# DLRM tower: eight of 26 embedding fields looked up by one-hot matmuls, the other gathers in bursts of three, set-up, moment and layer order rebuilt

## The chip, the cores and the metric

The kernel runs on one core of a Trainium2 chip. The metric is the device time of one execution in microseconds, lower is better; the median of several runs is compared.

## The reference

For a batch of 512 rows, 26 embedding rows of 32 floats each are fetched from 26 tables (1,000 to 125,000 rows long), and pass two layers of a compressed interaction network and a small multilayer perceptron, all in float32:

```python
e = stack([tbl_f[ids[:, f]] for f in range(26)], axis=1)        # (512, 26, 32)
x1 = einsum('bik,bjk,hij->bhk', e, e, W1) + b1                    # h = 128
x2 = einsum('bik,bjk,hij->bhk', x1, e, W2) + b2                   # h = 128
z = sum(concat([x1, x2], axis=1), axis=-1)                        # (512, 256)
h = maximum(concat([z, dense_ctx], axis=1) @ W_top1 + b_top1, 0)  # 272 -> 512
h = maximum(h @ W_top2 + b_top2, 0)                               # 512 -> 256
y = h @ W_top3                                                    # 256 -> 1
```

Only the sum over the 32 embedding columns is needed, so z is a cubic form of the 26 fields. The kernel uses that: it sums products of three fields over k ("moments") and multiplies them with folded weights.

## The kernel before

The batch is worked in 4 tiles of 128 rows. A tile's 26 fields are fetched by 26 indirect DMAs (gathers) that GpSimd issues one after the other (L242), each 128 rows of 128 bytes, into the one tile `rows`. The fields form three parts (`PARTS`: 13, 10 and 3 fields). Each gather of part p waits for `s_turn[p]`: VectorE must have taken that part of the tile before out of `rows`, since there is one buffer.

VectorE then (`half_a`, `half_b`) transposes each part in 32x32 blocks into `prod` (L616), so that partitions hold (row quad, k), and multiplies pairs of fields: 14 instructions for the pairs within the first 13 fields and the mixed groups (`products_a`, L771 to L777), 8 for the pairs of the other 13 (`products_b`, L788). ScalarE spreads the fields into the block-diagonal tile `diag` (`fill_diag`, L467), four copies for each part, one for each 32 partitions.

TensorE forms the moments (`moments`, L321 and L322): for each of 32 groups of four rows one matmul of 108 columns and one of 64, stationary `prod`, moving `diag`. Four groups make a step, eight steps a tile; two pairs of PSUM banks take turns, and ScalarE (`copy_moments`, L485 to L489) and VectorE (`steps`, L650) copy each step out into `t0` and `t1` before the step after the next may start. Then come Z2 (`z2_b`, `z2_second_chunk`, `z2_a`: 13, 8 and 13 matmuls of 128 columns) and Z1 (5 matmuls), and the layers `mlp1` (12 matmuls), `mlp2` (8) and `mlp3` (2). Layer 2 and 3 of a tile run behind the moments of the next one. Tiles 1 to 3 are run by a hardware loop (`Fori`) on TensorE and VectorE, tiles 1 and 2 on ScalarE, and GpSimd's loop has two rounds of two tiles.

Ahead of the first moments stands the set-up, done once: W2 is transposed (L275), multiplied with W1's symmetrised pairs (L281, 26 matmuls of 183 columns) and with its mixed block (L287, 26 of 169), the products are added into `folded` (L662, 95 additions on VectorE), and `folded` is transposed into `v0` and `v1` (L299, L302). It runs beside the gathers of tile 0.

What sets the order of the work is the order in which each engine's program is written, and semaphores. These lines of the loop matter for the prediction:

```python
for f in range(f0, f1):
    pool.indirect_dma_start(rows[:, f, :], None, tables[f], ...).then_inc(s_got[part], 16)
...
dve.wait_ge(s_mom, t * STEPS + STEPS)   # half_a: all moments of the tile before
fields_in(t, 0)
```

## Time and profile before

| | us |
|---|---|
| median of 3 runs | 188.49 (187.81 to 188.94) |
| span of the profiled execution | 269.0 |
| its TensorE, busy | 171.1 |
| its ScalarE, busy | 103.7 |
| its VectorE, busy | 94.1 |
| its GpSimd, busy | 109.4 (104 gathers: 108.7) |

The profile is of another execution than the three timed ones, and its span is 80.5 us longer than their median; its own time outside of the recording is not among the numbers. So its durations of single instructions and its waits have to be read apart. PE is TensorE, PEld its weight loads, DVE VectorE, ACT ScalarE, POOL GpSimd, SP the queue engine. A float32 matmul stands as two records.

### The profile page before, as it was taken

Reading aid. Unit: us, or ns where it says so; the run is one execution under the profiler, and the core shown is the slowest. Engines: PE = TensorE matmul, PEld = TensorE weight load, DVE = VectorE, ACT = ScalarE, POOL = GpSimd, SP = SyncE. Lnnn points to the kernel's source line nnn. Section 1 sums busy time; section 2 is a strip of 40 time slices with the busy share of each in tenths; the row PEclk is TensorE's granted clock in tenths of the full one; section 3 lists DMA queues with packets and bytes.
Section 4 is the critical chain, followed back from the end, with each engine's and each line's share of the span. In section 5 each row is a group of like instructions: output and inputs, shape, how many; then the busy total and the mean of one; then the engine's idle time right before and its main releaser. Section 6 shows DMA issues by size and latency. Waiting matters only on the chain.

```text
span 269.0 us, 3544 instructions
## 1 busy us (share of the span) xinstructions
PE 171.1 (64%) x1239; PEld 158.7 (59%) x1239; DVE 94.1 (35%) x370; ACT 103.7 (39%) x267; POOL 109.4 (41%) x110
## 2 busy tenths in 40 slices
PE   7900594209929388986300799954001999899997
PEld 7800583209729287976300789954002999888985
DVE  0576003210943086920000568500003569047200
ACT  1020330019595165494000462951003463966313
POOL 3778777720077400577774003877770000000000
PEclk9975598556997869996555599995555799999999
DMA  6700011000001000011000000001000000000000
GB/s 240 250 12 13 12 14 14 13 7 0 0 10 17 11 1 4 2 12 15 14 12 10 0 0 2 11 12 15 12 12 2 0 0 0 0 0 0 0 0 3
DMA packets 5729, 5.08 MB, mean 19 GB/s; under 512 B 2875, under 2 KB 5061, under 8 KB 5718
## 3 DMA queue, kind: packets, MB, share of 16 engines
q0 software_dynamic: 3328, 1.71, 4.7%
q1 hardware_dynamic: 1698, 2.34, 2.6%
q10 hardware_dynamic: 692, 0.89, 1.0%
q8 instruction: 6, 0.10, 0.2%
q14 instruction: 5, 0.04, 0.1%
HBM read 4.93 MB, written 0.00 MB: 18 GB/s over the span
## 4 chain that ended last, share of the span: by engine, by line
PE 35%; another core or an unknown queue 30%; ACT 15%; DVE 9%; issue 9%; POOL 0%; DVEq 0%; ACTq 0%; POOLq 0%
PE bank L321 9%; ACT diag L467 8%; PE bank L287 4%; DVE t L650 4%; PE bank L322 4%; PE bank L281 4%; PE bank L256 3%; PE bank L332 2%; DVE prod L771 2%; PE bank L372 1%; ACT w2t L432 1%; ACT t L486 1%; DVE prod L616 1%; PE bank L275 1%
## 5 line engine op out<-in xcount | busy, mean ns | idle before, releaser
L242 POOL DMA_INDIRECT rows<-in_tbl_dram,idx x104 | 108.7, 1045 | 91.1 <-DVE prod L616 57.4
L321 PE MATMUL bank<-diag,prod 128*128 128x108 f32 x256 | 60.7, 336 | 56.0 <-DVE t L650 44.3
L321 PEld LDWEIGHTS bank<-diag,prod 128*128 128x128 f32 x256 | 46.6, 227 | 59.5 <-issue 59.5
L650 DVE COPY t<-bank 13x64 f32<-13x64 f32 (+2 forms) x128 | 26.7, 209 | 108.6 <-ACT t L487 66.7
L322 PE MATMUL bank<-diag,prod 128*77 128x64 f32 x256 | 41.7, 249 | 0.3 <-issue 0.3
L322 PEld LDWEIGHTS bank<-diag,prod 128*77 128x77 f32 x256 | 36.8, 173 | 0.5 <-issue 0.5
L485 ACT COPY t<-bank 55x128 f32<-55x128 f32 x32 | 8.3, 259 | 71.9 <-remote 47.8
L467 ACT COPY diag<-prod 32x416 f32<-32x416 f32 (+2 forms) x48 | 33.4, 696 | 1.0
L287 PE MATMUL bank<-w1ab,w2t 128*128 128x169 f32 x52 | 16.0, 489 | 14.6 <-ACT folded L434 9.7
L287 PEld LDWEIGHTS bank<-w1ab,w2t 128*128 128x128 f32 x52 | 12.8, 278 | 17.5 <-ACT folded L434 10.4
L281 PE MATMUL bank<-w1s,w2t 128*128 128x183 f32 x52 | 10.8, 377 | 16.4 <-ACT w2t L432 15.6
L281 PEld LDWEIGHTS bank<-w1s,w2t 128*128 128x128 f32 x52 | 10.3, 233 | 16.9 <-ACT w2t L432 15.8
L788 DVE TENSOR_TENSOR prod<-prod 128x364 f32<-128x364 f32 x32 | 16.5, 536 | 0.8
L489 ACT COPY t<-bank 128x432 f32<-128x432 f32 x32 | 16.4, 512 | 0.0
L434 ACT COPY folded<-bank 128x366 f32<-128x366 f32 x13 | 5.8, 469 | 25.8 <-remote 11.7
L662 DVE TENSOR_TENSOR folded<-folded 128x6 f32<-128x6 f32 (+15 forms) x44 | 5.1, 177 | 27.4 <-ACT folded L434 13.2
L662 DVE TENSOR_TENSOR folded<-folded,ct 128x52 f32<-128x52 f32 (+13 forms) x51 | 11.6, 301 | 7.4 <-ACT ct L437 7.3
L349 PE MATMUL bank<-t,v 128*128 128x128 f32 x104 | 12.7, 279 | 0.0
L332 PE MATMUL bank<-t,v 128*128 128x128 f32 x104 | 12.4, 276 | 0.3 <-ACT t L489 0.3
L332 PEld LDWEIGHTS bank<-t,v 128*128 128x128 f32 x104 | 11.9, 192 | 0.6 <-ACT t L489 0.6
L349 PEld LDWEIGHTS bank<-t,v 128*128 128x128 f32 x104 | 11.9, 192 | 0.5
L363 PE MATMUL bank<-z,wt 128*128 128x128 f32 x64 | 9.0, 286 | 2.8 <-issue 2.1
(79 smaller groups left out, 186.3 us busy)
## 6 DMA issues: line engine op xcount, KB each, us to landing
rows<-in_tbl_dram,idx POOLq DMA_INDIRECT x104
wt<-in_W_top_dram SPq DMA_DIRECT2D x2, 512.0 KB
w<-in_L_rec_W_dram ACTq DMA_DIRECT2D x1, 832.0 KB
w<-in_L_rec_W_dram SPq DMA_DIRECT2D x1, 832.0 KB
w<-in_L_rec_W_dram SPq DMA_DIRECT2D x1, 338.0 KB
idx<-in_ids_dram SPq DMA_DIRECT2D x4, 13.0 KB
vec<-in_L_rec_b_dram ACTq DMA_DIRECT2D x2, 0.5 KB
dctx<-in_dense_ctx_dram ACTq DMA_DIRECT2D x1, 32.0 KB
```

The lines of the kernel that those rows point to most:

```text
L242: pool.indirect_dma_start(rows[:, f, :], None, tables[f], bass.IndirectOffsetOnAxis(ap=idx[i][:, f:f + 1], axis=0)).then_inc(s_got[part], 16)
L281: mm = nc.tensor.matmul(ps[:, i * PAIRS:(i + 1) * PAIRS], w2t[:, x0 + i, :], w1s[:], start=True, stop=True)
L287: mm = nc.tensor.matmul(ps[:, i * HALF * HALF:(i + 1) * HALF * HALF], w2t[:, lo + x0 + i, :], rhs, start=True, stop=True)
L321: nc.tensor.matmul(m0[:, g * P:g * P + JW * QUADS], prod[:, G, 0:P], mov, start=True, stop=True)
L322: mm = nc.tensor.matmul(m1[0:M1, g * J1 * QUADS:(g + 1) * J1 * QUADS], prod[:, G, P:P + M1], mov[:, JLOW * QUADS:], start=True, stop=True)
L332: nc.tensor.matmul(Z2[:, 0:P], v0[:, j, :], t0[:, j, :], start=j == HALF, stop=False)
L349: mm = nc.tensor.matmul(Z2[:, 0:P], v0[:, j, :], t0[:, j, :], start=False, stop=j == HALF - 1)
L467: nc.scalar.copy(diag[q, :, f0:f1, r], prod[q, :, col:col + f1 - f0]).then_inc(s_diag, 1)
L489: nc.scalar.copy(dst(t0, 0, P, slice(0, JW)), view(m0, P, slice(0, JW), P)).then_inc(s_e0, 1)
L650: ins = nc.vector.tensor_copy(t1[p0:p0 + HALF, GRAM + slot:GRAM + slot + nb, n].rearrange("p j (g r) -> p j g r", r=QUADS), m1[64:64 + HAL ...
L662: ins = nc.vector.tensor_tensor(dest, dest, term[second], ALU.add)
L788: return eng.tensor_tensor(dst, left, right, ALU.mult)
```

## The change

- **Fields.** The 26 fields are put in another order. Eight of them, with tables of 1,000 or 1,250 rows, are no longer gathered. Their tables are loaded whole into SBUF (`small`, 1.15 MB, in chunks of 128 rows). A one-hot matrix of the index's low seven bits is made once for all 512 rows (8 matmuls of 512 columns that broadcast the indices, 8 comparisons on VectorE). For each tile, 8 matmuls (5 of 256 columns, 3 of 320) pick a row from every chunk (`look_up`), and VectorE picks the chunk: six multiplications with a 0/1 mask out of PSUM and six reductions (`pick`).
- **Gathers.** 18 for each tile remain, 72 in all, each tile with a buffer of its own; nothing waits for VectorE any more. GpSimd waits after every three until they have landed.
- **Set-up.** W2 comes in the transposed layout and W1 in the pair layout from the host (layout only, the additions stay on chip), so the transposes of W2, W1 and the context and most small additions into `w1s` go. Loads on the SP and ACT queues grow: W1 in pair layout 0.53 MB, its transposed form 0.66 MB, `small` 1.15 MB.
- **Moments.** Steps of 8 groups (4 steps) on two sets of three banks. One operand of the pair products is read from PSUM (`factor`).
- **Order.** No hardware loops. Each tile runs moments, Z2, Z1 and all three layers before the next tile's moments. The copies of `v0`'s low half stand behind tile 0's moments. ScalarE spreads over all 128 partitions at once with a scale that is 1 on one quarter (4 instructions for each of parts 0 and 1; VectorE does part 2).

```diff
-GSTEP = 4
+GSTEP = 8
+ORDER = [2, 6, 7, 9, 0, 1, 3, 4, 5, 8, 10, 11, 12, 16, 23, 24, 25, 13, 14, 15, 17, 18, 19, 20, 21, 22]
+PARTS = [(0, 13, COL_A, 4), (13, 23, COL_B, 17), (23, 26, COL_B + 10, 23)]
+LATE_PART = 2
+BURST = 3
+SMALL = [0, 1, 2, 3, 13, 14, 15, 16]
+CHUNKS = [8, 8, 8, 8, 8, 10, 10, 10]
+MAXC = max(CHUNKS)
+SPLACE = [EMB * sum(CHUNKS[:e]) for e in range(len(SMALL) + 1)]
+PICKS = [(0, 2), (2, 4), (4, 5), (5, 6), (6, 7), (7, 8)]
...
-            with nc.gpsimd.Fori(0, TILES // 2) as u:
-                for i in range(2):
-                    pool.wait_ge(s_idx[i], u * 16 + 16)
-                    for part, (f0, f1, _) in enumerate(PARTS):
-                        pool.wait_ge(s_turn[part], u * 2 + i + 1)
-                        pool.sem_inc(s_go, 1)
-                        for f in range(f0, f1):
-                            pool.indirect_dma_start(
-                                rows[:, f, :], None, tables[f],
-                                bass.IndirectOffsetOnAxis(ap=idx[i][:, f:f + 1], axis=0)).then_inc(s_got[part], 16)
+            for t in range(TILES):
+                if t < 2:
+                    pool.wait_ge(s_idx[t], 16)
+                for part, (_, f1, _, g0) in enumerate(PARTS):
+                    for f in range(g0, f1):
+                        if f > g0 and (f - g0) % BURST == 0:
+                            pool.wait_ge(s_got[t][part], 16 * (f - g0))
+                        pool.indirect_dma_start(
+                            rows[t][:, f, :], None, tables[f],
+                            bass.IndirectOffsetOnAxis(ap=idx[:, t, f:f + 1], axis=0)).then_inc(s_got[t][part], 16)
+                    pool.wait_ge(s_got[t][part], 16 * (f1 - g0))
...
+            def broadcast():
+                pe.wait_ge(s_place, 1)
+                for e in range(len(SMALL)):
+                    nc.tensor.matmul(bank[e][:], with_dims(ident[0:len(SMALL), e:e + 1], (0, P)), placef[:],
+                                     start=True, stop=True).then_inc(s_bc, 1)
+            def look_up(t, picks):
+                for pick in picks:
+                    e0, e1 = PICKS[pick]
+                    ps = bank[ARRIVE[t > 0][pick]]
+                    if t == 0 and pick >= 2:
+                        pe.wait_ge(s_pick, pick - 1)
+                    elif t and pick == 5:
+                        pe.wait_ge(s_pick, t * len(PICKS) + 1)
+                    for e in range(e0, e1):
+                        c = slice(SPLACE[e] - SPLACE[e0], SPLACE[e + 1] - SPLACE[e0])
+                        mm = nc.tensor.matmul(ps[:, c], onehot[:, e, t * P:(t + 1) * P],
+                                              small[:, SPLACE[e]:SPLACE[e + 1]], start=True, stop=True)
+                    mm.then_inc(s_em, 1)
...
+            def keep_clock(t):
+                pe.wait_ge(s_turn[1], t + 1)
+                for _ in range(FILL):
+                    nc.tensor.matmul(bank[2][:, 0:P], ident[:], ident[:], start=True, stop=True)
+            for t in range(TILES):
+                if t:
+                    pe.wait_ge(s_y, t)
+                if t == TILES - 1:
+                    keep_clock(t)
+                moments(t)
+                if t < TILES - 1:
+                    pe.wait_ge(s_e0, t * STEPS + 3)
+                    pe.wait_ge(s_eg, t * STEPS + 3)
+                    look_up(t + 1, (0, 1))
+                pe.wait_ge(s_e0, t * STEPS + STEPS)
+                pe.wait_ge(s_eg, t * STEPS + STEPS)
+                if t == 0:
+                    for q in range(DONE["v1"], len(SETUP)):
+                        make(q)
+                    pe.wait_ge(s_sf, len(SETUP))
+                    pe.wait_ge(s_vec, 32)
+                    pe.wait_ge(s_wt, 48)
+                if t < TILES - 1:
+                    look_up(t + 1, (2, 3, 4))
+                z2_low()
+                if t < TILES - 1:
+                    look_up(t + 1, (5,))
+                z2_high()
+                if t == 0:
+                    pe.wait_ge(s_z1w, 1)
+                z1()
+                if t < TILES - 1:
+                    pe.wait_ge(s_pick, (t + 2) * len(PICKS))
+                layer1(t)
+                layer2(t)
+                layer3(t)
...
-            def fill_diag(t, parts):
-                act.wait_ge(s_mom, t * STEPS + STEPS)
-                for part in parts:
-                    f0, f1, col = PARTS[part]
-                    act.wait_ge(s_turn[part], t + 2)
-                    for r in range(QUADS):
-                        q = slice(32 * r, 32 * r + 32)
-                        nc.scalar.copy(diag[q, :, f0:f1, r], prod[q, :, col:col + f1 - f0]).then_inc(s_diag, 1)
+            def spread(t, part):
+                f0, f1, col, _ = PARTS[part]
+                act.wait_ge(s_turn[part], t + 1)
+                for r in range(QUADS):
+                    ins = nc.scalar.activation(diag[:, :, f0:f1, r], prod[:, :, col:col + f1 - f0], ACT.Identity,
+                                               scale=quad[:, r:r + 1])
+                ins.then_inc(s_diag, 1)
+            for q in range(DONE["v1"]):
+                take(q)
+            for part in range(LATE_PART):
+                spread(0, part)
+            for t in range(TILES):
+                evict(t)
+                if t == 0:
+                    for q in range(DONE["v1"], len(SETUP)):
+                        take(q)
+                    act.wait_ge(s_vec, 32)
+                if t < TILES - 1:
+                    spread(t + 1, 0)
+                act.wait_ge(s_z2, t + 1)
+                nc.scalar.activation(z[1][:], Z2[:, 0:P], ACT.Identity, bias=b2x32[:, 0:1]).then_inc(s_z2s, 1)
+                act.wait_ge(s_z1, t + 1)
+                nc.scalar.copy(z[0][:], Z1[:, 0:P]).then_inc(s_z1s, 1)
+                relu1(t)
+                relu2(t)
+                copy_y(t)
+                if t < TILES - 1:
+                    spread(t + 1, 1)
...
+            for e in range(len(SMALL)):
+                dve.wait_ge(s_bc, e + 1)
+                nc.vector.tensor_scalar(onehot[:, e, :], bank[e][:], placef_of[:, 0:1], None,
+                                        ALU.is_equal).then_inc(s_oh, 1)
...
+            def pick(t):
+                if t == 0:
+                    dve.wait_ge(s_ch, 1)
+                for i, (e0, e1) in enumerate(PICKS):
+                    n, cs = e1 - e0, CHUNKS[e0]
+                    width = n * EMB * cs
+                    dve.wait_ge(s_em, t * len(PICKS) + i + 1)
+                    if t or i:
+                        dve.wait_ge(s_sum, t * len(PICKS) + i)
+                    nc.vector.tensor_tensor(
+                        picked[:, 0:width].rearrange("p (f k c) -> p f k c", f=n, c=cs),
+                        bank[ARRIVE[t > 0][i]][:, 0:width].rearrange("p (f k c) -> p f k c", f=n, c=cs),
+                        with_dims(chosen[:, t, e0, 0:1], (MAXC, n), (0, EMB), (1, cs)), ALU.mult).then_inc(s_pick, 1)
+                    dve.wait_ge(s_pick, t * len(PICKS) + i + 1)
+                    nc.vector.tensor_reduce(rows[t][:, SMALL[e0]:SMALL[e0] + n, :],
+                                            picked[:, 0:width].rearrange("p (f k c) -> p f k c", f=n, c=cs),
+                                            mybir.AxisListType.X, ALU.add).then_inc(s_sum, 1)
...
+                nc.vector.tensor_copy(factor[:, :, first:first + n], prod[:, :, col:col + n]).then_inc(s_fac, 1)
...
-        eng.tensor_tensor(prod[:, :, col:col + n], field(o, n), field(o + d, n), ALU.mult)
+        eng.tensor_tensor(prod[:, :, col:col + n], factor[:, :, o:o + n], field(o + d, n), ALU.mult)
```

The gathers on GpSimd, in `before` (a loop body that runs twice) and then in the change; the numbers in brackets are the semaphores waited for, `s_turn` being VectorE's transposes and `s_got` the gathers' own landing:

```order
L242 DMA rows<-in_tbl_dram,idx 128x32 [waits s_turn0]
L242 DMA rows<-in_tbl_dram,idx 128x32 x12
L242 DMA rows<-in_tbl_dram,idx 128x32 [waits s_turn1]
L242 DMA rows<-in_tbl_dram,idx 128x32 x9
L242 DMA rows<-in_tbl_dram,idx 128x32 [waits s_turn2]
L242 DMA rows<-in_tbl_dram,idx 128x32 x2
```

```order
L248 DMA rows<-in_tbl_dram,idx 128x32 [waits s_idx0]
L248 DMA rows<-in_tbl_dram,idx 128x32 x2
L248 DMA rows<-in_tbl_dram,idx 128x32 [waits s_got0_0]
L248 DMA rows<-in_tbl_dram,idx 128x32 x2
L248 DMA rows<-in_tbl_dram,idx 128x32 [waits s_got0_0]
L248 DMA rows<-in_tbl_dram,idx 128x32 x2
```

The wait for VectorE is gone, and one for the three gathers before has come.

TensorE behind the moments of a tile, in the loop of `before` and then in the change (tile 1; `t` and `v` are moments and folded weights, `w1c`/`z1w` the weights of Z1):

```order
L372 MATMUL bank<-h,wt 128x128 x4
L332 MATMUL bank<-t,v 128x128 [waits s_e0]
L332 MATMUL bank<-t,v 128x128 x12
L340 MATMUL bank<-t,w1sT 128x128
L343 MATMUL bank<-t,w1c 128x128 [waits s_eg]
L343 MATMUL bank<-t,w1c 128x128 x3
...
L337 MATMUL bank<-t,v 128x128 x8
L349 MATMUL bank<-t,v 128x128 x13
```

```order
L277 MATMUL bank<-small,onehot 128x256 x3
L277 MATMUL bank<-small,onehot 128x256 [waits s_eg,s_e0]
L277 MATMUL bank<-small,onehot 128x320 x2
L338 MATMUL bank<-t,v 128x128 x13
L277 MATMUL bank<-small,onehot 128x320 [waits s_pick]
L342 MATMUL bank<-t,v 128x128 x13
...
L374 MATMUL bank<-h,wt 128x128
L382 MATMUL bank<-h,vec 1x128 [waits s_h2] x2
L331 MATMUL bank<-diag,prod 128x108 [waits s_late,s_pick,s_diag,s_pb,s_pa,s_y]
```

The look-ups of the next tile have come in between, and layers 2 and 3 of the same tile now stand ahead of the next tile's moments, which wait for `s_y`.

ScalarE between two tiles, in the loop of `before` and then in the change:

```order
L514 COPY y<-bank 1x128
...
L467 COPY diag<-prod 32x32x13 [waits s_turn0]
L467 COPY diag<-prod 32x32x13 x3
...
L495 COPY z<-bank 128x128 [waits s_z]
L467 COPY diag<-prod 32x32x10 [waits s_turn1,s_mom]
L467 COPY diag<-prod 32x32x10 x3
```

```order
L493 ACTIVATE diag<-prod,quad 128x32x13 [waits s_turn0]
L493 ACTIVATE diag<-prod,quad 128x32x13 x3
L525 ACTIVATE z<-bank,b2x 128x128 [waits s_z2]
L527 COPY z<-bank 128x128 [waits s_z1]
L500 ACTIVATE h<-bank,vec 128x128 [waits s_l1] x4
L505 ACTIVATE h<-bank,vec 128x128 [waits s_l2] x2
L509 COPY y<-bank 1x128 [waits s_l3]
L493 ACTIVATE diag<-prod,quad 128x32x10 [waits s_turn1]
L493 ACTIVATE diag<-prod,quad 128x32x10 x3
```

The spread of part 1 now stands behind the last copy (`y`) of the tile before.

## Rows read from the trace of the kernel before

**Rows 1.** Spans and clock of all cores

```profile
core 0: 269.0 us, clock 0.797
```

**Rows 2.** Page part 2: busy tenths in 40 slices of the span

```profile
PE   7900594209929388986300799954001999899997
...
POOL 3778777720077400577774003877770000000000
```

**Rows 3.** Page part 4: shares of the chain that ended last

```profile
PE 35%; another core or an unknown queue 30%; ACT 15%; DVE 9%; issue 9%; POOL 0%; DVEq 0%; ACTq 0%; POOLq 0%
```

**Rows 4.** The chain, its two longest gaps: start us, us, what

```profile
126.92 20.83 another core or an unknown queue
...
183.90 21.32 another core or an unknown queue
```

**Rows 5.** Timeline of POOL: start us, us, engine line op [idle before <-releaser]

```profile
4.55 1.14 POOL L242 DMA_INDIRECT rows<-in_tbl_dram,idx  x1 [3.17 <-issue]
...
38.53 0.95 POOL L242 DMA_INDIRECT rows<-in_tbl_dram,idx  x1 [0.30 <-issue]
...
111.38 3.00 POOL L242 DMA_INDIRECT rows<-in_tbl_dram,idx  x1 [0.30 <-issue]
...
143.61 0.94 POOL L242 DMA_INDIRECT rows<-in_tbl_dram,idx  x1 [0.30 <-issue]
165.46 4.26 POOL L242 DMA_INDIRECT rows<-in_tbl_dram,idx  x1 [20.91 <-DVE prod L616]
```

**Rows 6.** Page part 5: the gathers; busy, mean ns, idle before

```profile
L242 POOL DMA_INDIRECT rows<-in_tbl_dram,idx x104 | 108.7, 1045 | 91.1 <-DVE prod L616 57.4
```

**Rows 7.** Waits in total: us, times, longest

```profile
POOL rows L242 <- issue: 33.7, 101, 3.2
```

**Rows 8.** Timeline of SP: the index reload that waits for tile 0's gathers

```profile
41.08 52.13 SPq L224 DMA_DIRECT2D idx<-in_ids_dram  x2
```

**Rows 9.** Timeline of ACT: filling of `diag` for tile 1

```profile
113.41 3.95 ACT L467 COPY diag<-prod 32x416 f32<-32x416 f32 x4
...
117.67 3.15 ACT L467 COPY diag<-prod 32x320 f32<-32x320 f32 x4
...
121.12 1.49 ACT L467 COPY diag<-prod 32x96 f32<-32x96 f32 x4
```

**Rows 10.** The chain: transposes, cold and warm moment groups, Z2 to layer 3 of the last tile

```profile
75.43 1.64 PE bank L299 x13
...
150.66 0.51 PE bank L321 x2
151.41 0.51 PE bank L321 x2
...
248.50 0.26 PE bank L321 x2
248.88 0.26 PE bank L321 x2
...
251.50 2.90 PE bank L332 x26
...
261.31 1.08 PE bank L359 x8
...
267.20 0.26 ACT y L514
```

**Rows 11.** Stretches: PE, PEld, DVE, ACT, POOL busy (instructions), PEclk, DMA share, GB/s

```profile
6.00:10.00 4.00, 4.00 (x31) 3.86 (x30) 2.82 (x30) 0.00 (x0) 3.08 (x4) 1.00 1.02 362
...
35.00:41.00 6.00, 5.22 (x34) 4.94 (x33) 0.43 (x5) 1.75 (x4) 4.51 (x5) 1.00 0.10 14
```

**Rows 12.** Timeline of DVE: additions into `folded`, then tile 1's transposes and products

```profile
67.27 5.46 DVE L662 TENSOR_TENSOR folded<-folded,ct 128x65 f32<-128x65 f32 x26 [7.32 <-ACT ct L437]
...
108.41 0.91 DVE L616 STREAM_TRANSPOSE prod<-rows 128x416 f32<-128x416 f32 x1
...
113.48 0.73 DVE L616 STREAM_TRANSPOSE prod<-rows 128x320 f32<-128x320 f32 x1
...
114.79 1.43 DVE L788 TENSOR_TENSOR prod<-prod 128x364 f32<-128x364 f32 x3
```

More of the change, by code:

```diff
@@ L78 @@
 M1 = 64 + HALF
+CROSS = HALF * HALF
 GRAM = J1 // 2
@@ L96, with dlrm_tower @@
 MT2 = N_TOP2 // P
-def dlrm_tower(nc, dense_ctx, ids, tables, W_top1, b_top1, W_top2, b_top2, W_top3, W1, b1, W2, b2, out):
+RING = [0, 1, 2, 3, 4, 5]
+SETUP = [("fold", j, 2) for j in range(0, FIELDS, 2)]
+SETUP += [("ctA", x, min(3, HALF - x)) for x in range(0, HALF, 3)]
+SETUP += [("ctB", x, min(3, HALF - x)) for x in range(0, HALF, 3)]
+SETUP += [("v0", j, min(4, FIELDS - j)) for j in range(HALF, FIELDS, 4)]
+SETUP += [("v1", x, min(4, J1 - 1 - x)) for x in range(0, J1 - 1, 4)]
+SETUP += [("v0", j, min(4, HALF - j)) for j in range(0, HALF, 4)]
+DONE = {kind: q + 1 for q, (kind, first, n) in enumerate(SETUP)}
+def dlrm_tower(nc, io, tables, out):
     with ExitStack() as ctx:
@@ L323, in moments, with z2_low @@
+                        mm = nc.tensor.matmul(m1[0:M1, a1:a1 + J1 * QUADS], prod[:, G, P:P + M1],
                                               mov[:, JLOW * QUADS:], start=True, stop=True)
                     mm.then_inc(s_mom, 1)
-                    if s < len(between):
-                        make(between[s])
-            def z2_b(t):
-                pe.wait_ge(s_e0, t * STEPS + STEPS)
+            def z2_low():
+                for j in range(HALF):
+                    nc.tensor.matmul(Z2[:, 0:P], v0[:, j, :], t0[:, j, :], start=j == 0, stop=False)
@@ new lines, in layer1 @@
+                    nc.tensor.matmul(L1[m][:, 0:P], wt1c[:, chunk(m)], dctx[:, t * P:(t + 1) * P], start=True, stop=False)
+                for m in range(MT1):
+                    nc.tensor.matmul(L1[m][:, 0:P], wt1[:, 1, chunk(m)], z[1][:], start=False, stop=False)
+                pe.wait_ge(s_z1s, t + 1)
+                for m in range(MT1):
+                    mm = nc.tensor.matmul(L1[m][:, 0:P], wt1[:, 0, chunk(m)], z[0][:], start=False, stop=True)
+                    mm.then_inc(s_l1, 1)
@@ new lines, in fields_in @@
+            def fields_in(t, part):
+                f0, f1, col, g0 = PARTS[part]
+                n = f1 - f0
+                dve.wait_ge(s_got[t][part], 16 * (f1 - g0))
+                dve.wait_ge(s_sum, t * len(PICKS) + NEEDS[part])
+                nc.vector.transpose(prod[:, :, col:col + n].rearrange("p g f -> p f g"),
+                                    rows[t][:, f0:f1, :]).then_inc(s_turn[part], 1)
+                dve.wait_ge(s_turn[part], t + 1)
+                if part == 1:
+                    dve.wait_ge(s_pa, t + 1)
+                first = f0 % HALF
+                nc.vector.tensor_copy(factor[:, :, first:first + n], prod[:, :, col:col + n]).then_inc(s_fac, 1)
+                if part == LATE_PART:
+                    for r in range(QUADS):
+                        q = slice(32 * r, 32 * r + 32)
+                        ins = nc.vector.tensor_copy(diag[q, :, f0:f1, r], prod[q, :, col:col + n])
+                    ins.then_inc(s_late, 1)
@@ L676, in _ @@
             add(cross, 1, True)
+            pick(0)
+            half_a(0)
             half_b(0)
+            dve.wait_ge(s_sf, DONE["ctB"])
             cross = cross_b(folded, ct[1])
-            dve.wait_ge(s_sf, done["ctB"])
-            third = -(-len(cross) // 3)
-            steps(0, [(cross[x * third:(x + 1) * third], second, second == 1 and x == 2)
-                      for second in range(2) for x in range(3)])
-            with nc.vector.Fori(1, TILES) as t:
+            add(cross, 0, False)
+            bands(0, 0, 2)
+            add(cross, 1, True)
+            bands(0, 2, STEPS)
+            for t in range(1, TILES):
+                pick(t)
                 half_a(t)
                 half_b(t)
-                steps(t)
+                bands(t)
 def with_dims(ap, *dims):
@@ L795 @@
 def kernel(**inputs):
-    import numpy as _np
     import concourse.bacc as _bacc
-    from concourse import mybir as _mybir
     from concourse.bass_utils import run_bass_kernel_spmd as _run
     nc = _bacc.Bacc("TRN2", target_bir_lowering=False, num_devices=1)
+    laid = layouts(inputs)
+    laid.update({f"tbl_{i}": np.asarray(inputs[f"tbl_{ORDER[i]}"]) for i in range(FIELDS) if i not in SMALL})
     arrays, aps = {}, {}
-    for name in NAMES:
-        a = _np.ascontiguousarray(inputs[name])
+    for name, a in laid.items():
+        a = np.ascontiguousarray(a)
@@ L811 @@
+    out = nc.dram_tensor("out_0_dram", (BATCH, 1), F32, kind="ExternalOutput").ap()
+    dlrm_tower(nc, aps, [aps.get(f"tbl_{i}") for i in range(FIELDS)], out)
     r = _run(nc, [arrays], core_ids=[0])
```

615 lines of the change are left out of this document (281 added, 334 removed).

## The prediction

> **What bounds the kernel now.** I began with the spans and the page's slices: the recorded span is 269.0 us [rows 1], 80.5 more than the median of 188.49, and in the loop TensorE idles in two stretches of two whole slices, both beside a busy POOL [rows 2]. The shares of the chain [rows 3] name the surplus: 30% of 269.0 us is "another core or an unknown queue", that is 80 us, and the two longest pieces are 20.8 and 21.3 us at the first two rounds of TensorE's loop [rows 4]. Without them 189 us are left, which is the median. The first of these gaps ends at 147.8, 3 us after the last gather issued before it (143.61 + 0.94) [rows 5], and the third round, beside which nothing is gathered, has none. So I take these gaps to belong to the recording, and leave them out of both sums.
>
> What bounds the runs that are timed is then a question of two chains. **The gathers:** they start at 4.55 [rows 5]; 104 of them are busy 108.7 us [rows 6], and 33.7 us lie in the 0.3 us steps between them [rows 7]: 142.4 us with nothing waited for. The last of a tile lands 1.6 us after its end (38.53 + 0.95, reload at 41.08) [rows 5, 8]. Then part 2 is transposed (0.3), its spread takes 1.5 [rows 9], and the last tile's moments to the end of the span take 33.3 (from 235.7, by the busy slices the only undisturbed tile, to 269.0). Sum 4.6 + 142.4 + 1.6 + 0.3 + 1.5 + 33.3 = 183.7. **The compute chain** of a tile is half_a, the spread and the moments, some 29 us, against 26 x 1.37 = 35.6 for its gathers. So GpSimd sets the pace; 4.8 us of the median stay without a name.
>
> **Gathers, after.** 72 instead of 104, in 24 bursts. A burst is 3 x 0.95 + 2 x 0.30 + 1.6 for landing + 0.1 = 5.15 us, all 24 are 124 us, and the last lands at 129. The landing is bounded by 1.4 us and, for three in flight beside 5 MB of loads, by some 3 us: 119 to 163. Tile 3 needs its last field only at about 155 (below), so this comes off the path. The longest gathers (3.00 at 111.38, 4.26 at 165.46) lie beside VectorE's products (from 108.41 and 164.7) [rows 5, 12]; over all they add 104 x 0.095 = 10 us to before's chain, and what they add after is slack.
>
> On that the Trainium skill, SBUF — State Buffer, SBUF: two separate sides, says that GpSimd is locked out of a port pair that it shares with VectorE while that reads two SBUF operands. By that rule the move of `factor` to PSUM ends the long gathers; the rows agree with the first half, and none has an operand in PSUM. The sum below stays the same either way.
>
> **Start to the first moments.** The weights come in pair layout: loads ran at 362 GB/s [rows 11], and 0.2 MB more puts `w1s` at 7.1 us. The 8 broadcasts of 512 columns cost 4 x 0.223 = 0.89 each (2.90 / 13 for 128 columns [rows 10]), from 3.9 to 11.0. 26 folds at 0.307 (5.22 / 17 [rows 11]) end at 19.0, copied at 19.5; the 26 mixed ones and two look-ups run beside VectorE. VectorE adds: 44 low terms 4.5, the first mixed ones 5.5 [rows 12], to 29.5. Then what is new on the path: the six picks read 2,240 elements twice; at 0.48 us for 364 [rows 12] that is 5.9, and 12 semaphore steps of 0.07 make 6.7: 36.2. half_a 5.1 (108.41 to 113.48) [rows 12] and 0.45 for `factor`: 41.8. Transposing part 1 takes 0.7, its four spreads 3.2 [rows 9]. The first moments start at **46** (42 to 51: both ends from the picks at half and at double, and the loads). W2's transposes, 3 us on TensorE, are gone but were hidden beside the loads.
>
> **A tile, after.** Everything on TensorE now stands in a row:
> - moments: a warm group takes 0.385 (248.50 to 248.88 [rows 10]), 32 make 12.3; by the old steps they took 14.6, so the wider steps save 2.3.
> - copying out the last step: 2.1; the first two look-up pairs hide in it.
> - the other four look-ups, (256 + 3 x 320) / 128 x 0.223 = 2.1.
> - Z2 and Z1: 9.3 (251.50 to 261.31, less 0.5 of layer 3 [rows 10]).
> - layers 1 to 3 up to `y`: 6.2 (261.31 to 267.46 [rows 10]). Before, layers 2 and 3 lay behind the next moments, and their waits cost nothing.
> - ScalarE's spread of part 1, behind `y`: 4 x 0.79 + 0.1 = 3.3 [rows 9]. TensorE waits for it.
>
> Together 35.3. VectorE's picks, half_a and half_b (6.7 + 5.6 + 5.5) hide under Z and the layers, 21 us; if they slip by over 3, they come on top. Tile 0 adds 13 late transposes and their copies (1.6 [rows 10] + 1.0) and, behind 12 us of idleness, a cold start: a group takes 0.75 (150.66 to 151.41 [rows 10]) for some 6.5 groups, 2.4. Tile 0: 40.3. Tiles 1 and 2: 70.6. Each of their 3.3 us waits may drop the clock to 1.2 GHz; that costs 0 or 2.4 each, I take one. The last tile, whose wait the twelve filling matmuls bridge: 12.3 + 2.1 + 9.3 + 6.2 + 1.5 for the output = 31.4.
>
> Sum: 46 + 40.3 + 70.6 + 2.4 + 31.4 = 190.7, against 183.7 by the same way of counting before. Of before's nameless 4.8 us I carry over none, since part belongs to loops and long gathers, and forecast **191 us**, 1.3% more. The change takes the gathers off the path and puts an unbroken line of TensorE, VectorE and ScalarE there that is 7 us longer.
>
> The rule against leaving out the loops' share: the Trainium skill, Runtime: NRT & Kernel Launch, Instruction fetch mechanics, says that a taken branch breaks the sequential prefetch of code and stalls the engine. By it the nameless 4.8 us are three loop entries, and the unrolled program has none: 190.7. Without it they may come along: 195.5. The rows show gaps at two of three entries, but only beside gathers [rows 4].
>
> **The rivals.**
> 1. *The line is shorter than its rows, and the change is faster.* Before, the compute chain is hidden, so the median does not vouch for its durations, and the recording may stretch them. At the rate of plain matmuls a group's 172 columns take 0.30 instead of 0.385: 11 us less over four tiles, 180. It decides from a tile of 34 us downward. For it speaks that the recording adds 80 us elsewhere; against it, that the gather chain from the same record gives 183.7 of 188.5. 32%.
> 2. *The serial line slips further*: TensorE waits for picks, for z copies behind the spread of part 0 on ScalarE, or cold clocks after each wait, and the nameless 4.8 come along: 195.5 to 200. 16%.
> 3. *The bursts bind after all.* It takes over 6.3 us for a burst, a landing of 2.8. At 7 us the last field lands at 173, and 1.6 + 31.4 later it ends: 206. Against it: 1.6 measured behind 26 gathers in a row [rows 8]. 7%.
> That the gathers were never on the path is a rival too: then before spent more than 4.8 us in stalls, nothing is gained by freeing them, and the new line's sum, which does not lean on them, stays. It moves no number and has no share.
>
> **How the numbers follow.** A measurement of this kernel tells about 0.5% (0.9 us) from no change. The forecast's own case, 188 to 194, holds 45%, of it 12 within 187.5 to 189.4 and 33 above. Faster: rival 1, 32%. Slower: 33 + 16 + 7 = 56%. The range leaves out rival 3, a part of 2 and the best end of 1: 180 to 200.
>
> **What would show it.** TensorE's line without gaps of over 4 us from the first moments (at 46) on; a period of 35 to 38 us from moments to moments; POOL ending at about 130; no wait of L331 for a gather; a pick phase of 6 to 7 us. Wrong would be: periods under 34 (rival 1), L331 or VectorE's transpose waiting for `rows` in the last tile (rival 3), unknown gaps that are no shorter than before.

## The result, and the profile after

The changed kernel takes **203.68 us** (median of four runs, 202.16 to 205.12) against 188.15 (187.78 to 188.94) of the kernel before, measured beside it: a ratio of 1.081, 95% interval 1.075 to 1.088. The direction was forecast, the size was not: 191 us, at most 200. The recorded execution took 205.12 us, of which 203.3 lie in its span. Single executions of these kernels can come out far longer (of the kernel before, timed beside the experiments, one took 241.7 and one 792 us), and the ratios leave such executions out. Spans and clock, and the page's slices of TensorE, GpSimd and the clock:

```profile
core 0: 203.3 us, clock 0.933
```

```profile
PE   6999999791069989993999999759999998996995
...
POOL 5253555655557653555455355550000000000000
PEclk9999999997558999999589999966999999999999
```

Against [rows 1, 2]: the two empty stretches of TensorE are gone, GpSimd is half busy and done at two thirds of the span, and the clock dips three times. The shares of the chain that ended last:

```profile
PE 64%; DVE 26%; issue 4%; ACT 4%; DVEq 0%
```

Nothing is left on a queue or unknown [rows 3]. That much of the forecast holds: gathers are off the path, and TensorE with VectorE stands there. (In tiles 1 and 2 the chain names VectorE's products ahead of the moments. But for tile 2 they end at 133.1, while ScalarE's spread, which TensorE waits for too, runs from 131.5 to 134.3, just ahead of the moments at 134.47. So there it is the spread, and VectorE is hidden by about 1 us.) What this line costs is in the chain, in order of time (start us, us, what):

```profile
4.83 14.02 PE bank L263 x16
18.84 11.08 PE bank L295 x52
29.94 0.47 ACT folded L449
30.51 2.45 DVE folded L659 x25
...
48.20 0.88 DVE prod L610
...
57.58 0.73 PE bank L331 x2
...
96.86 0.73 PE bank L331 x2
...
134.47 0.73 PE bank L331 x2
...
169.25 2.94 PE bank L389 x24
...
186.29 3.17 PE bank L338 x26
```

The first two rows are the surprise. The eight broadcasts (L263, sixteen records of 512 columns) hold TensorE for 14.0 us, the folds behind them (L295) for 11.1. The first moments start at 57.58, the next tiles at 96.86, 134.47 and 172.2 (169.25 + 2.94, behind the filler). So the span is 57.6 + 39.3 + 37.6 + 37.7 + 31.1. The filler is the twelve matmuls of `keep_clock` (L389). Of the first groups in tiles 1 and 2 the stretches read (PE, PEld, DVE, ACT, POOL busy, clock, DMA share, GB/s):

```profile
96.80:103.00 6.20, 6.14 (x33) 6.17 (x34) 0.00 (x0) 0.00 (x0) 3.22 (x5) 0.50 0.06 11
134.40:140.60 6.20, 6.13 (x33) 6.16 (x34) 0.00 (x0) 0.00 (x0) 0.99 (x2) 0.50 0.05 8
```

Both tiles begin at the 1.2 GHz level, behind a wait of 3.1 us. Last, GpSimd's timeline at the start and its line in the page:

```profile
5.90 0.94 POOL L248 DMA_INDIRECT rows<-in_tbl_dram,idx  x1 [0.30 <-issue]
11.78 0.94 POOL L248 DMA_INDIRECT rows<-in_tbl_dram,idx  x1 [4.94 <-DMA rows<-in_tbl_dram,idx]
...
23.48 0.94 POOL L248 DMA_INDIRECT rows<-in_tbl_dram,idx  x1 [1.66 <-DMA rows<-in_tbl_dram,idx]
```

```profile
L248 POOL DMA_INDIRECT rows<-in_tbl_dram,idx x72 | 73.0, 1013 | 61.3 <-DMA rows<-in_tbl_dram,idx 45.2
```

A burst's end costs 1.5 to 1.7 us in 18 of the 23 waits. The two beside the loads of the first 18 us cost 4.9 and 3.1, and three later ones 2.1 to 2.9. Together they are 45.2 us. The last gather starts at 134.8, 30 us before VectorE transposes what it brings (165.2).

### The profile page after: what moved, and what is told of

Read it like the earlier page. It is cut to its first block, busy times and chain, and to the rows that moved or that the text cites. A ratio compares the mean times of both kernels' runs of the same rounds, so it can differ in the third digit from the quotient of the medians.

```text
span 203.3 us, 3318 instructions
## 1 busy us (share of the span) xinstructions
PE 176.5 (87%) x1261; PEld 157.2 (77%) x1261; DVE 120.7 (59%) x390; ACT 80.5 (40%) x188; POOL 73.7 (36%) x79
## 4 chain that ended last, share of the span: by engine, by line
PE 64%; DVE 26%; issue 4%; ACT 4%; DVEq 0%
PE bank L331 19%; PE bank L332 9%; PE bank L263 7%; PE bank L295 5%; DVE folded L659 5%; PE bank L338 4%; PE bank L277 4%; DVE prod L787 4%; DVE prod L772 3%; PE bank L342 3%; DVE picked L595 3%; DVE prod L610 3%; DVE rows L600 2%; PE bank L345 2%; PE bank L374 2%
## 5 line engine op out<-in xcount | busy, mean ns | idle before, releaser
L248 POOL DMA_INDIRECT rows<-in_tbl_dram,idx x72 | 73.0, 1013 | 61.3 <-DMA rows<-in_tbl_dram,idx 45.2
L648 DVE COPY t<-bank 13x128 f32<-13x128 f32 (+1 forms) x64 | 16.8, 263 | 41.8 <-PE bank L332 41.1
L332 PE MATMUL bank<-diag,prod 128*77 128x64 f32 x256 | 40.3, 243 | 0.0
L493 ACT ACTIVATE diag<-prod,quad 128x416 f32<-128x416 f32 (+1 forms) x32 | 25.0, 936 | 27.8 <-DVE prod L610 27.8
L477 ACT COPY t<-bank 55x256 f32<-55x256 f32 (+2 forms) x48 | 14.1, 293 | 38.6 <-PE bank L332 38.2
L277 PE MATMUL bank<-small,onehot 128*128 128x256 f32 (+1 forms) x64 | 17.9, 410 | 1.2 <-ACT v L455 0.8
L595 DVE TENSOR_TENSOR picked<-bank,chosen 128x320 f32<-128x320 f32 (+2 forms) x24 | 13.1, 547 | 5.3 <-PE bank L277 3.4
L485 ACT COPY t<-bank 128x432 f32<-128x432 f32 x32 | 14.8, 515 | 0.0
L277 PEld LDWEIGHTS bank<-small,onehot 128*128 128x128 f32 x64 | 11.2, 190 | 4.5 <-DVE picked L595 1.2
L787 DVE TENSOR_TENSOR prod<-bank,prod 128x364 f32<-128x364 f32 x32 | 14.6, 528 | 0.1
L263 PE MATMUL bank<-placef,ident 8*128 8x512 f32 x16 | 14.0, 1066 | 0.5 <-DVE placef L558 0.5
L338 PEld LDWEIGHTS bank<-t,v 128*128 128x128 f32 x104 | 12.2, 192 | 2.4 <-ACT t L485 2.0
L338 PE MATMUL bank<-t,v 128*128 128x128 f32 x104 | 12.4, 276 | 1.8 <-ACT t L485 1.8
L600 DVE TENSOR_REDUCE rows<-picked 128x32 f32<-128x320 f32 (+2 forms) x24 | 13.0, 542 | 0.8
L295 PEld LDWEIGHTS bank<-w1s,w2t 128*128 128x128 f32 x52 | 10.9, 243 | 1.5 <-DVE onehot L566 1.5
L263 PEld LDWEIGHTS bank<-placef,ident 8*128 8x128 f32 x16 | 5.1, 329 | 8.1 <-issue 7.3
```

The source lines that it names most:

```text
L248: pool.indirect_dma_start(rows[t][:, f, :], None, tables[f], bass.IndirectOffsetOnAxis(ap=idx[:, t, f:f + 1], axis=0)).then_inc(s_got[t][p ...
L263: nc.tensor.matmul(bank[e][:], with_dims(ident[0:len(SMALL), e:e + 1], (0, P)), placef[:], start=True, stop=True).then_inc(s_bc, 1)
L277: mm = nc.tensor.matmul(ps[:, c], onehot[:, e, t * P:(t + 1) * P], small[:, SPLACE[e]:SPLACE[e + 1]], start=True, stop=True)
L295: mm = nc.tensor.matmul(ps[:, i * PAIRS:(i + 1) * PAIRS], w2t[:, x0 + i, :], w1s[:, 0:PAIRS], start=True, stop=True)
L332: mm = nc.tensor.matmul(m1[0:M1, a1:a1 + J1 * QUADS], prod[:, G, P:P + M1], mov[:, JLOW * QUADS:], start=True, stop=True)
L338: nc.tensor.matmul(Z2[:, 0:P], v0[:, j, :], t0[:, j, :], start=j == 0, stop=False)
```

## The experiments

Twelve runs, on several chips; each ratio is against the kernel before, run beside it. Runs 2 and 8 leave eight fields out of the result and serve only to time the rest.

**1. The kernel before, unchanged, recorded again (e0_before).**

> The kernel before, unchanged, recorded once more. If the two waits of 21 us on an unknown queue belonged to the one recorded execution (theory A), this recording has neither, its gathers end at 140 to 150 us, and its chain of waits ends in the last tile's gather-to-output stretch as in the first recording, with a span within 3 us of its own time. If they belong to the kernel (theory B), two such waits of 15 to 25 us appear again on the queue of GpSimd or of the loads.

188.7 us, 187.33 to 190.58, ratio 1.002 (0.995 to 1.008). Span, shares of the chain, and the chain before the last tile:

```profile
core 0: 185.9 us, clock 0.917
```

```profile
POOL 56%; PE 18%; issue 18%; DMA 3%; ACT 2%; POOLq 1%; DVE 0%; ACTq 0%
```

```profile
4.80 1.14 POOL rows L242
...
142.52 2.24 DMA rows<-in_tbl_dram,idx
144.78 0.75 DVE prod L616
...
146.51 0.77 ACT diag L467
...
151.37 0.39 PE bank L321 x2
```

Theory A: no gap of 20 us in this recording, and 56% of the chain is gathers. They run from 4.80 to 147.3 (the last starts at 146.3), where the prediction's sum had 147.0; the last tile's moments start at 151.4 (sum: 150.4) and the rest takes 34.5 us (sum: 33.3). The path differs a little from the sum's: the chain leaves GpSimd at the last gather of part 1 (142.52) and goes on over ScalarE's spreads, not over the very last gather. The recorded run took 187.65 us, 1.75 more than its span. So of the 4.8 us that I had left nameless, about 2 are small terms inside the span and about 2 lie outside it, in every kernel here.

**2. Only 18 gathers per tile in the kernel before (e4_before18).** Eight factor rows are zeros; the index reload waits for the 18.

```diff
+FIRST = [4, 17, 23]
-                        for f in range(f0, f1):
+                        for f in range(FIRST[part], f1):
```

> The kernel before with the eight fields of the change neither gathered nor picked (their columns are zeros, so these fields are left out of the result): 72 unbroken gathers, everything else as before. Theory A (before was bound by its 104 gathers, 142 us of 184): the gathers take 44 us less, the compute chain of about 29 us a tile takes over, 173 to 179 us. Rival B (before was bound by its compute chain): within 1% of 188. Rival C (before was bound by other engines being held up while gathers ran): a fall in proportion to the gathers, 170 us or less.

173.39 us (171.26 to 180.11), ratio 0.919 (0.907 to 0.930): theory A. Its moments start at 42.2, 78.1, 108.1 and 138.1, so 30.0 us per inner tile. The gathers did bind the kernel before, by 14 us, and its compute chain is about as short as the prediction's "some 29 us".

**3. The broadcasts over 128 rows (e1_wide).** The eight rows of places are padded with zeros.

```diff
-        placef = sb("placef", [len(SMALL), BATCH])
+        placef = sb("placef", [P, BATCH])
-with_dims(ident[0:len(SMALL), e:e + 1], (0, P)), placef[:],
+with_dims(ident[:, e:e + 1], (0, P)), placef[:],
```

> The change with the index broadcast on all 128 rows: `placef` is padded with zeros to 128 partitions and the stationary column has 128 rows, so the result is the same. Theory A (the eight broadcast matmuls took 1.75 us each, because TensorE ran at its 1.2 GHz level all through them and into the folds, and it stayed there because only 8 of its 128 rows were in use): the first broadcasts still take 1.75, the later ones about 0.88, the folds 0.31 from their start; the 14.0 and 11.1 us become about 10 and 8, less 0.4 for the longer memset: 197 to 198 us. Rival B (a float32 matmul of 512 columns takes 1.75 us whatever the clock): 203 to 205 us, folds as before.

195.98 us (195.46 to 196.19), ratio 1.044 (1.035 to 1.052): 7.7 us back, a little more than theory A had. The chain:

```profile
5.21 8.93 PE bank L263 x16
14.14 8.07 PE bank L295 x52
```

Sixteen records of the same 512 columns take 8.9 us in place of 14.0, and the folds 8.1 in place of 11.1. First moments at 49.85.

**4. 24 warming matmuls in place of 6 (g1_warm24).** That leaves the rows at eight and takes away the cold beginning.

```diff
-WARM = 6
+WARM = 24
```

> The changed kernel with 24 warming matmuls ahead of the broadcasts in place of 6 (as many as the kernel before had), nothing else. They end at about 9 us, so the broadcasts start some 4.5 us later. Theory A (the eight-row broadcasts were slow because they began at the 1.2 GHz level and that level was never left in them: it is the warming that was too short): each record then takes about 0.43 us, all sixteen about 7, they end at about 16.5 in place of 18.8, the folds take 8.2 in place of 11.1, and the whole is about 5 us shorter, 197 to 200 us. Theory B (matmuls over eight of the 128 rows don't hold the 2.4 GHz level: the rows are the cause): most records still take 0.85 to 0.88 us, the sixteen 12 us or more, they end at 21 or later, and the whole is 1 to 5 us longer than 203.7.

205.0 us (204.86 to 205.53), ratio 1.088 (1.079 to 1.096). Stretches (PE, PEld, DVE, ACT, POOL busy, clock, DMA share, GB/s):

```profile
5.00:8.00 3.00, 3.00 (x29) 3.00 (x28) 0.70 (x1) 0.31 (x1) 1.50 (x2) 1.00 1.03 415
8.00:11.00 3.00, 3.00 (x10) 1.44 (x10) 1.38 (x2) 0.00 (x0) 0.00 (x0) 1.00 1.03 391
11.00:12.00 1.00, 1.00 (x3) 0.45 (x2) 0.87 (x2) 0.00 (x0) 0.26 (x1) 0.57 0.93 346
12.00:19.00 7.00, 7.00 (x9) 2.41 (x8) 3.00 (x4) 0.00 (x0) 3.35 (x4) 0.50 0.74 240
19.00:24.00 5.00, 5.00 (x16) 4.44 (x15) 3.95 (x25) 1.30 (x3) 2.62 (x4) 0.50 0.08 10
24.00:26.00 2.00, 2.00 (x12) 2.00 (x12) 1.07 (x3) 1.03 (x3) 1.61 (x2) 0.80 0.10 16
```

Theory B, and the row shows it happen. TensorE is at the 2.4 GHz level when the broadcasts start at 8.35; within them, with no idle time at all (1.00 of 1.00 us from 11 on, 7.00 of 7.00 from 12 on), the granted clock falls to the 1.2 GHz level and stays there until the folds, which start at 19.57, have run for some 5 us. The sixteen take 11.3 us, which at 0.43 and 0.85 a record, the two levels of these runs, is about six fast and ten slow ones. So **fp32 matmuls over eight of the 128 rows do not hold the clock**, here after 7 us of matmuls over all 128. The Trainium skill, TensorE: Matmul & The Clock Gate, Part 1: The HAM clock gate, has the gate follow how busy the engine has been; by that rule a busy 7.00 of 7.00 should keep the upper level, and this row does not agree. Why is open; runs 3 and 4 only show that the level differs with the rows.

**5. The broadcasts in bf16 (e6_bf16).** Places are below 128, so they stay exact.

```diff
-        placef = sb("placef", [len(SMALL), BATCH])
+        placef = sb("placef", [len(SMALL), BATCH], mybir.dt.bfloat16)
-with_dims(ident[0:len(SMALL), e:e + 1], (0, P)), placef[:],
+with_dims(identb[:, e:e + 1], (0, P)), placef[:],
```

> The changed kernel with the eight broadcasts in bf16 (placef and the one-hot stationary, values up to 127 are exact). Theory A (the set-up's TensorE time is on the path): the broadcasts take about 3 to 4 us in place of 14.0, the compares of VectorE (8 x 0.75 us) then set their pace at about 7, first moments at about 47 to 50 us, and the whole 192 to 197 us. Theory B (the first moments wait for something that lands or is computed late besides): less than 4 us come back, 200 us or more.

195.67 us (194.7 to 205.15), ratio 1.039 (1.028 to 1.049): theory A. TensorE's timeline:

```profile
5.02 1.90 PE L264 MATMUL bank<-placef,identb 8*128 8x512 bf16 x8 [0.67 <-DVE placef L562]
9.77 10.68 PE L296 MATMUL bank<-w1s,w2t 128*128 128x183 f32 x52 [2.85 <-DMA w2t<-in_w2t_dram]
```

Broadcasts 1.9 us instead of 14.0, first moments at 48.13, 9.5 earlier. The 12.1 us that the broadcasts lose would have made it 45.5, but TensorE now waits 2.85 us for the weights of the folds. These start at the 1.2 GHz level again and take 10.7 us, for 11.1.

**6. Filler matmuls ahead of tiles 1 and 2 too (e2_fill).**

```diff
-                if t == TILES - 1:
+                if t:
                     keep_clock(t)
```

> The change with the twelve filling matmuls of the last tile also ahead of the moments of tiles 1 and 2. Theory A: the 3.2 us wait for the spread drops the clock in both tiles, eight moment groups take 0.74 instead of 0.385, 2.9 us each; with the filler these go: 203.7 - 5.8 = 198 us. Rival B (the slow groups come from something else than the idle time ahead, or the filler is in the way): 203 to 205 us.

The four runs, 195.5 to 200.8 (median 199.72), agree too badly for an interval, so this one is read from its trace (recorded: 199.54, span 197.7):

```profile
92.83 2.94 PE bank L389 x24
...
127.41 2.94 PE bank L389 x24
...
162.01 2.94 PE bank L389 x24
...
179.08 4.80 PE bank L338 x26
```

From filler to filler a tile takes 34.6 us in place of 37.6 and 37.7: each cold start costs 3.0, as in theory A. But in the last tile Z2 (L338), which took 3.17, now starts cold and takes 4.80. Why it is cold here and not in the changed kernel, behind the same filler and moments, is open.

**7. No bursts in the changed kernel (e3_unbroken).**

```diff
-                        if f > g0 and (f - g0) % BURST == 0:
-                            pool.wait_ge(s_got[t][part], 16 * (f - g0))
-                    pool.wait_ge(s_got[t][part], 16 * (f1 - g0))
```

> The change without any wait between gathers, 72 in a row. The gaps of 20 us in the trace of the kernel before ended with its gathers. Theory A (they belong to that one recorded execution, and the bursts are worth nothing): the gathers end at about 95 instead of 136, the line of TensorE stays, time within 1% of 203.7, recorded span within 3 us of it. Rival B (unbroken gathers hold the other engines up in every execution, though less than recorded, and the bursts prevent that): gaps in TensorE's or VectorE's line while the gathers run, time 208 us or more.

204.03 us (202.6 to 204.24), ratio 1.085 (1.076 to 1.095): theory A. The last gather starts at 96.5 in place of 134.8, and the time is the same. The bursts neither cost nor bring anything here.

**8. New order, 18 gathers, nothing picked (e8_nopick18).** Broadcasts, one-hot rows and picks are gone; eight factor rows are zeros.

```diff
-            broadcast()
...
-                if t < TILES - 1:
-                    look_up(t + 1, (2, 3, 4))
...
+                link(nc.vector.memset(rows[t][:, 0:4, :], 0.0))
```

> The changed kernel with 18 gathers per tile, without bursts, broadcasts and picks; it leaves out eight of the 26 fields, whose factor rows are zeros. Theory A: with the first moments at about 40, then 37, 35.5 and 35.5 us for three tiles and 31 for the last, 179 to 183 us: the new order of moments and layers is itself 6 to 10 us slower than the old one with the same 18 gathers (173.4 us), and the picks and their set-up are the other 20 or so of the changed kernel's 203.7. Theory B (the new order is no worse, all of the loss is the picks): 171 to 175 us.

183.28 us (182.74 to 184.93), ratio 0.976 (0.967 to 0.986), 0.3 us above theory A's range. The first moments start at 42.8, and the four tiles take 37.3, 34.2, 34.4 and 32.7 us. Two things follow. The picks with their set-up cost 20.4 us of the 203.7; of the 21.9 between the spans, 14.8 lie ahead of the first moments and 8.7 in tiles 0 to 2, less 1.6 in the last. And the new order, at the same 18 gathers, is 9.9 us slower than the old one of run 2: both start their moments at 42, but an inner tile takes 34.3 us instead of 30.0. "New order" here means all that came with it (steps, spreads, `factor`, layers ahead of the next moments); no run takes these apart.

**9. New order, all 26 fields gathered, no bursts (e5_gatherall).** The edit is that of run 8 with every part's gathers from its first field on, and no zeros:

```diff
-PARTS = [(0, 13, COL_A, 4), (13, 23, COL_B, 17), (23, 26, COL_B + 10, 23)]
+PARTS = [(0, 13, COL_A, 0), (13, 23, COL_B, 13), (23, 26, COL_B + 10, 23)]
```

> The changed kernel with all 26 fields gathered again and no bursts: no one-hot rows, no broadcast, no picks; the new order of set-up, moments and layers stays. Theory A (the picks cost the changed kernel more than they save it, because the TensorE work of their set-up stands ahead of the first moments): first moments at about 40 us in place of 57.6, then 35 to 38 us per tile until the 104 gathers bind: the last one ends at about 147 to 152, so 181 to 188 us. Theory B (fewer gathers are what the new order needs): the gathers bind in every tile, 190 us and more, no better than 3% under the changed kernel's 203.7.

**182.81 us** (182.2 to 183.65), ratio **0.972 (0.964 to 0.979)**: it computes everything, and beats both kernels. Theory A has the time; its "until the 104 gathers bind" is answered below. The gathers (shortest, median and longest in ns; first and last start), and the chain at tile 2:

```profile
L244 POOL DMA_INDIRECT rows<-in_tbl_dram,idx x104: 940/944/3087, 4.6 to 138.5; - x104
```

```profile
106.03 2.29 DMA rows<-in_tbl_dram,idx
...
108.34 0.36 DVE prod L565
...
110.10 3.65 DVE prod L740 x8
...
114.06 0.44 PE bank L323 x2
```

The chain still runs over the gathers up to tile 2, and yet the time is that of run 8: with 104 gathers or 72, the moments start at 42.6 or 42.8, 79.8 or 80.0, 114.1 or 114.3. In this order the gathers bind by almost nothing. Against run 1 the last one starts at 138.5 in place of 146.3. The gathers themselves are shorter by 7.5 us (103.5 busy against 111.0), with the same 0.3 us steps between them. The traces show which ones. Lines of GpSimd and VectorE, from run 1 and then from run 9:

```profile
68.22 3.37 POOL L242 DMA_INDIRECT rows<-in_tbl_dram,idx  x1 [0.30 <-issue]
68.66 1.14 DVE L773 TENSOR_TENSOR prod<-prod 128x960 f32<-128x960 f32 x1
```

```profile
45.64 3.09 POOL L244 DMA_INDIRECT rows<-in_tbl_dram,idx  x1 [0.30 <-issue]
44.78 3.12 DVE L614 TENSOR_TENSOR folded<-folded,ct 128x169 f32<-128x169 f32 x13
```

In run 1 four gathers take over 3 us, one in each tile (25.04, 68.22, 98.73 and 136.54), and each lies beside the products L771 to L777, which read both operands from SBUF. In run 9 two do (45.64 and 52.78), and both lie beside additions into `folded`; beside the products, which now read `factor` from PSUM, no gather takes over 1.3 us.

**10. The same in bursts (e5b_gather_burst).**

```diff
+                        if f > g0 and (f - g0) % BURST == 0:
+                            pool.wait_ge(s_got[t][part], 16 * (f - g0))
+                    pool.wait_ge(s_got[t][part], 16 * (f1 - g0))
```

> All 26 fields gathered in the new order, but in bursts of three as the changed kernel has them. Theory A (bursts cost a landing each, and were free in the changed kernel only because 72 gathers leave GpSimd idle): about 1.6 us more for each of 35 or so burst ends, the last gather at about 190 us in place of 138.5, the whole 230 to 240 us. Theory B (waiting removes the contention that lengthens gathers and so pays for itself): under 200 us.

234.51 us, ratio 1.245 (1.228 to 1.263). Its gathers and their waits:

```profile
L246 POOL DMA_INDIRECT rows<-in_tbl_dram,idx x104: 938/944/2734, 5.9 to 196.0; - x104
...
  DMA rows<-in_tbl_dram,idx: 68.7, 39
```

39 waits of 1.76 us each, as in theory A; the gathers are busy 102.8 us (103.5 in run 9), so waiting shortened them by next to nothing. The bursts were affordable in the changed kernel only because 32 gathers had gone.

**11. Run 9 with every cold start filled (f1_gather_keep).** WARM = 30, and `keep_clock` ahead of all four tiles.

> All 26 fields gathered without bursts in the new order (182.8 us), with the twelve filler matmuls ahead of every tile's moments and 30 warming ones ahead of the folds in place of 6. Theory A (what is left is cold starts and the gathers between them): the folds take about 8.2 us in place of 10.3, the first eight group pairs of tiles 0 to 2 are at 0.385 us in place of 0.74, but tiles 1 and 2 still start where their last gather has landed (about 80 and 114 us), so only the last tile starts 2 to 3 us earlier: 179 to 182 us. Theory B (the gathers bind nowhere in this order, as the equal time with 18 gathers would have it): all four gains count, 172 to 176 us.

182.68 us (182.21 to 184.32), ratio 0.969 (0.959 to 0.978): the same as run 9. Theory A's range is missed by a little and theory B's is far off, and the reason is neither. Tile 0 gained nothing: its first groups are cold here too (0.73 us for the first record pair, at 44.20), 6.3 us behind the filler's end. Stretches of tile 1, first of this kernel, then of run 9:

```profile
81.50:90.00 8.50, 8.50 (x90) 8.50 (x90) 4.46 (x14) 3.42 (x10) 6.50 (x7) 1.00 0.10 15
...
95.60:100.50 4.90, 4.89 (x29) 4.89 (x30) 4.83 (x16) 3.48 (x4) 3.68 (x5) 0.65 0.06 12
```

```profile
80.00:84.00 4.00, 4.00 (x29) 4.00 (x29) 1.27 (x3) 0.00 (x0) 3.09 (x4) 0.64 0.10 14
...
95.60:100.50 4.90, 4.74 (x42) 4.74 (x43) 4.83 (x16) 3.63 (x5) 3.68 (x5) 1.00 0.09 13
```

In tiles 1 and 2 the cold stretch has moved, not gone: the moments are warm from the start, and Z2 behind them runs at 0.65 of full clock and takes 4.80 us (3.17 in run 8's tiles 1 and 2). In run 6 the look-ups stood between moments and Z2, and Z2 stayed at 2.90.

**12. bf16 broadcasts, fillers and no bursts together (e7_best).** The edits of runs 5, 6 and 7, with the filler ahead of tile 0 too.

> The changed kernel with three edits together: broadcasts in bf16, the filler matmuls ahead of every tile's moments, no bursts. Theory A (the terms stand one behind another and add up): 195.7 us less 2.9 for each of the cold starts of tiles 0 to 2 is 187 us, between 185 and 189: level with the kernel before, and still 2% or more behind the version that gathers everything. Theory B (a tile's start then waits for VectorE or ScalarE, which make its operands): less than 4 us come back, 192 us or more.

189.72 us (189.37 to 220.62), ratio 1.006 (1.002 to 1.010), so level with the kernel before; 0.7 us above theory A's range. The eight bf16 broadcasts took 3.6 us here, 0.45 each, for 1.9 in run 5. Tiles 1 and 2 take 34.6 us (3.0 less each), tile 0 gained nothing, since its filler's operands are there long before its moments: 3.8 us lie between. Even with these three edits, the version that picks stays 7 us behind the one that gathers.

## Why the prediction was right or wrong

**What bounded the kernel before: right.** The two gaps belonged to that recording (run 1); the gathers set the pace (run 2), and the sum's 183.7 stands against a span of 185.9.

**Gathers, after: right.** Off the path; mostly 1.6 us for a landing; the last one ends at 135.7 (its landing was forecast for 129). The lower bound there, 119, leaves out the start at 4.6 us and should have been 123. The rule of the Trainium skill, SBUF — State Buffer, SBUF: two separate sides, changed no number then, and the traces agree with it now: no long gather lies beside the products any more (run 9), and those of 1.96, 2.37 and 2.52 us that the changed kernel still has (36.56, 61.87, 68.30) lie beside additions into `folded` with both operands in SBUF. So "ends the long gathers" came true for those beside the products, and not for these. No run moved `factor` back alone, so its part in run 9's gain is argued and not shown.

**Start to the first moments: the step that failed**, 57.6 in place of 46, nearly all of the 12.6 us by which the span exceeds the sum.
- *The 8 broadcasts at "0.89 each"* took 1.75: 14.0 us, from 4.83 to 18.84, where the sum had 3.9 to 11.0. +7.8, of which 0.9 is the later start. I scaled a row of warm matmuls over 128 partitions [rows 10] by the number of columns, and took for granted that the clock would be there: the windows of before read 1.00 [rows 11]. It was at the 1.2 GHz level, and eight rows kept it there (runs 3 and 4). After's own record has 1.00 for this stretch as well, against its durations (last section).
- *26 folds at 0.307*, also a warm price: 11.1 in place of 8.0, +3.1. Run 3 has 8.1.
- VectorE's additions: 10.2 for the forecast 10.5. The picks: 8.1 for 6.7, of it 1.0 waiting for look-ups (L277), +1.4. half_a, part 1 and its spread: 9.4 for 9.8.

**A tile, after: right to 1 us but for the cold starts.** Tile 0 took 39.3 (forecast 40.3), the last 31.1 (31.4), a warm group 0.385 as said. Tiles 1 and 2 took 37.6 and 37.7 for 35.3 each and one cold start between them. Both paid it, eight groups at 0.36 more, 2.9 each (forecast 2.4, once). "I take one" was a choice between 0, 1 and 2 with no row behind it: +2.3.

**The nameless 4.8 us.** Carrying none was wrong by 1.8, the share outside the span. By the rule of the Trainium skill, Runtime: NRT & Kernel Launch, Instruction fetch mechanics, it belonged to loops, which the traces do not bear out: the looped kernel of run 1 and the unrolled one lie 1.75 and 1.8 us above their spans, and the chain of neither has an unknown gap. No run here shows a cost of the loops.

**The rivals.** *1, a shorter line:* refuted, a group takes 0.385 at the upper clock in every trace. *2, the line slips further, 195.5 to 200:* the right side, and cold clocks after each wait were in it; but the largest part stood in the set-up, where no rival looked. *3, bursts bind:* refuted; a burst took 5.0 to 5.1 us in most cases and 5.5 on average, for a forecast of 5.15; run 10 shows the kernel in which they would have. That the gathers were never on the path is refuted by run 2.

**What the change got wrong** is thus more than the broadcasts. Without any picks the new order gathers all 26 fields in 182.8 us, 5.3 less than before: that was the part worth having. The picks relieve gathers that, in this order, hardly bind any more, and put 20 us on engines that do.

## What to carry to other kernels

Price a matmul from a row of its own rows-by-columns shape and at the clock that it will find; a warm row scaled by columns is a lower bound. Ask of each part of a large change whether the resource it relieves still binds once the other parts are in: here the new order by itself left the gathers hardly binding, and the picks then cost 20 us to relieve them. A filler pays only if what follows the filled stretch keeps the clock; otherwise the cold stretch turns up at the next pause.

## What the runs showed of the hardware that was not expected

- Eight-row fp32 matmuls let the granted clock fall from the 2.4 to the 1.2 GHz level with TensorE busy throughout (run 4: 1.00 when they start at 8.35, 0.50 from 12 us on); with 128 rows, mostly of zeros, it rises (run 3: sixteen records in 8.9 us). The same eight-row broadcasts in bf16 took 0.24 us each in run 5 and 0.45 in run 12, the two levels again; whether they would hold the upper one for longer was not tried.
- A recorded clock of 1.00 early in an execution is not to be trusted where the durations speak against it. The changed kernel's stretch beside run 4's (same columns as above) has 10 records of these broadcasts in 7 us at a recorded 1.00, run 4 has 9 in 7 us at 0.50; the work and the pace are the same:

```profile
12.00:19.00 7.00, 7.00 (x10) 2.37 (x9) 3.13 (x5) 0.00 (x0) 3.25 (x4) 1.00 0.74 241
```

- A wait of 2.9 us ahead of the folds (run 5) and waits of 3.1 us ahead of the moments are followed by the 1.2 GHz level, in the changed kernel at once, in run 9 after three groups of tile 1.
- Gathers of 128 rows take 0.94 us on GpSimd, but one that falls beside VectorE's work on two SBUF operands took up to 3.6 us (25.04 in run 1). Beside products with one operand in PSUM none took over 1.3 us (run 9).
- What made the 80 us of gaps in the first recording of the kernel before is open. They did not return in run 1, nor in any other recording here.
